# An attention layer in fp16 pairs: the low part of the attention result moves from VectorE to GpSimd

## What is computed

```
q, k, v = heads(x @ Wq + bq), heads(x @ Wk + bk), heads(x @ Wv + bv)
scores  = einsum('bhqd,bhkd->bhqk', q, k) / sqrt(32)
scores  = where(mask == 0, -inf, scores)
attn    = softmax(scores)
out     = einsum('bhqk,bhkd->bhqd', attn, v)      # back to (64, 128, 512)
result  = layernorm(x + out @ Wo + bo)            # eps 1e-5
```

## Time and profile before

| what | value |
|---|---|
| median of 3 runs | 910.06 us (909.27 to 911.1) |
| profiled execution | 910.95 us, its span 909.2 us |
| mean granted clock of PE | 0.986 of full speed |
| busy PE, DVE, ACT, POOL | 96%, 89%, 76%, 30% of the span |
| low part of the attention result on DVE (L463) | 44.7 us, 64 times, 698 ns |
| low part of x on POOL (L230) | 70.0 us, 60 times, 1166 ns |

### The profile page before, as it was taken

The page is one execution under the profiler, slowest core; times in us unless marked ns, Lnnn a source line. Parts: engine busy times, 40 slices in busy tenths (PEclk is TensorE's granted clock), DMA queues, the critical chain, the costliest instruction groups (busy, mean ns, idle before and its releaser), DMA issues.

```text
span 909.2 us, 34909 instructions
## 1 busy us (share of the span) xinstructions
PE 870.0 (96%) x11784; PEld 606.9 (67%) x11784; DVE 809.6 (89%) x3449; ACT 689.1 (76%) x1745; POOL 273.0 (30%) x386
## 2 busy tenths in 40 slices
PE   6989999999999999999999999999999999999954
PEld 4666667777666777666777666777766677766632
DVE  5789899989899999999999999998989999999984
ACT  5787788777787887777877778877778788777761
POOL 0122233332323333323333223333232333322222
PEclk9999999999999999999999999999999999999967
DMA  8277887876678877678877677787667887667863
GB/s 301 60 148 135 140 175 172 179 160 151 129 166 179 176 161 148 149 143 176 179 167 169 125 151 168 172 178 167 142 137 159 179 177 161 149 148 149 149 140 93
DMA packets 362287, 143.33 MB, mean 158 GB/s; under 512 B 340752, under 2 KB 344848, under 8 KB 361872
## 3 DMA queue, kind: packets, MB, share of 16 engines
q1 hardware_dynamic: 362256, 142.93, 73.3%
HBM read 42.21 MB, written 16.78 MB: 65 GB/s over the span
## 4 chain that ended last, share of the span: by engine, by line
PE 71%; DVE 21%; issue 4%; DMA 2%; DVEq 1%; ACT 0%; SPq 0%; POOL 0%; POOLq 0%; ACTq 0%
PE proj_ps L610 57%; PE score_ps L610 7%; PE av_ps L610 6%; DVE masked L497 6%; DVE p_pair L484 5%; DVE stats L526 3%; DVE y L523 3%; DVE qT_lo L477 1%; DVE v_parts L470 1%; DMA pT<-p_pair 1%; DVE minus_max L497 1%; DVE inv_sum L506 1%; DMA w_land<-weights 1%; DVE attn L511 0%; DMA aT<-a_pair 0%
## 5 line engine op out<-in xcount | busy, mean ns | idle before, releaser
L412 ACT ACTIVATE probs<-masked,minus_max 128x128 f32<-128x128 f32 x1024 | 326.9, 391 | 170.3 <-DVE minus_max L497 165.9
L497 DVE CUSTOM_DVE_ANT_0 masked<-score_ps,mask 128x128 f32<-128x128 f32 x1024 | 236.9, 287 | 48.2 <-PE score_ps L610 29.8
L484 DVE SCALAR_TENSOR_TENSOR p_pair<-probs,p_pair 128x512 f16<-128x512 f32 x256 | 196.6, 768 | 1.3 <-ACT p_pair L422 1.1
L422 ACT ACTIVATE p_pair<-probs 128x512 f16<-128x512 f32 x256 | 161.3, 630 | 13.3
L610 PE MATMUL proj_ps<-wo_hi,aT 128*128 128x512 f16 x512 | 166.4, 387 | 2.4 <-DMA aT<-a_pair 1.5
L230 POOL TENSOR_TENSOR xT_lo<-xT_raw,xT_hi 128x512 f16<-128x512 f32 x60 | 70.0, 1166 | 309.3 <-ACT xT_hi L375 309.3
L610 PE MATMUL proj_ps<-xT_hi,wq_hi 128*128 128x256 f16 x512 | 141.3, 276 | 11.3 <-DVE wq_lo L578 7.9
L610 PE MATMUL proj_ps<-xT_hi,wk_hi 128*128 128x256 f16 x512 | 140.3, 274 | 2.6 <-DVE qT_lo L477 2.4
L610 PE MATMUL proj_ps<-xT_lo,wq_hi 128*128 128x256 f16 x512 | 140.7, 275 | 0.0
L610 PE MATMUL proj_ps<-xT_hi,wq_lo 128*128 128x256 f16 x512 | 140.7, 275 | 0.0
L610 PE MATMUL proj_ps<-xT_hi,wk_lo 128*128 128x256 f16 x512 | 139.7, 273 | 0.0
(11 more groups left out here) (58 smaller groups left out, 1523.0 us busy)
## 6 DMA issues: line engine op xcount, KB each, us to landing
xT_raw<-x_cols SPq DMA_DIRECT2D x32, 512.0 KB, 4.3
x_in<-x_rows SPq DMA_DIRECT2D x32, 512.0 KB, 5.0
out<-y SPq DMA_DIRECT2D x64, 256.0 KB, 2.6
adj_in<-adj SPq DMA_DIRECT2D x32, 128.0 KB, 2.4
pT<-p_pair SPq DMA_TRANSPOSE x256, 3.1
w_land<-weights SPq DMA_DIRECT2D x2, 1024.0 KB, 7.7
w_land<-weights SPq DMA_DIRECT2D x4, 256.0 KB, 5.5
x_res<-weights SPq DMA_DIRECT2D x1, 1024.0 KB, 9.6
```

What stands on the lines that cost most here:

```text
L412: ins = act.activation(probs[s % 2][:, j * S:(j + 1) * S], masked[s % 2][:, j], ACT.Exp, bias=minus_max[s % 2][:, j:j + 1], scale=-1.0)
L422: act.activation(p_pair[s % NT][:, 0:HW], probs[s % 2][:], ACT.Copy, scale=P_UP).then_inc(p_hi_done, 1)
L484: dve.scalar_tensor_tensor(out=p_pair[s % NT][:, HW:2 * HW], in0=probs[s % 2][:], scalar=P_UP, in1=p_pair[s % NT][:, 0:HW], op0=ALU.mult, ...
L497: ins = dve.tensor_tensor_reduce(masked[s % 2][:, j], score_ps[j][:, s % HC], mask[par][:, s // KC], -EXP_SCALE, 3.0e38, ALU.add, ALU.min, ...
```

## The change

GpSimd makes the low part of the attention result. On GpSimd it stands at s=0 for the first graph and at s=4 for the second, and the second residual moves from s=4 to s=5. The constant column holds 1 instead of 16, so that the attention result comes out 16 times larger, and both of its parts are made without a multiplication: ACT copies without a scale, GpSimd subtracts.

```
+            def low_part_attn(g, b):
+                pool.wait_ge(a_hi_done, batch(g, b) + 1)
+                pool.tensor_tensor(a_pair[b][:, D:2 * D], attn[b][:], a_pair[b][:, 0:D],
+                                   ALU.subtract).then_inc(a_lo_done, 1)
...
                     if s == 1 and at_least(g, 2):
                         normalize(g - 2, 1)
+                    if s == 0 and at_least(g, 1):
+                        low_part_attn(g - 1, 0)
+                    if s == 4 and at_least(g, 1):
+                        low_part_attn(g - 1, 1)
...
-                    if s == 4:
+                    if s == 5:
                         residual(g, 1, par, k)
...
+            low_part_attn(LAST, 0)
             normalize(LAST - 1, 1)
+            low_part_attn(LAST, 1)
...
-                act.activation(a_pair[b][:, 0:D], attn[b][:], ACT.Copy, scale=UP).then_inc(a_hi_done, 1)
+                act.activation(a_pair[b][:, 0:D], attn[b][:], ACT.Copy).then_inc(a_hi_done, 1)
...
-            def low_part_attn(g, b):
-                dve.wait_ge(a_hi_done, batch(g, b) + 1)
-                dve.scalar_tensor_tensor(out=a_pair[b][:, D:2 * D], in0=attn[b][:], scalar=UP, in1=a_pair[b][:, 0:D],
-                                         op0=ALU.mult, op1=ALU.subtract).then_inc(a_lo_done, 1)
...
-                    if s in (2, 4) and at_least(g, 1):
-                        low_part_attn(g - 1, s // 4)
...
-                dve.memset(v_parts[i][:, :, :, V_ONE:VC], UP).then_inc(ones_made, 1)
+                dve.memset(v_parts[i][:, :, :, V_ONE:VC], 1.0).then_inc(ones_made, 1)
```

More of the change, by code:

```diff
@@ L597, in _ @@
             head_norm(LAST, SLOTS - 4)
-            low_part_attn(LAST, 0)
             y_and_moments(LAST - 1, 1, 1 - LAST % 2)
@@ L602, in _ @@
             head_norm(LAST, SLOTS - 1)
-            low_part_attn(LAST, 1)
             y_and_moments(LAST, 0, LAST % 2)
```

## The result

| | before | after |
|---|---|---|
| median of the runs, us | 910.52 (909.27 to 911.1, 4 runs) | 939.11 (936.53 to 940.44, 4 runs) |
| profiled execution, us | 910.95 | 940.44 |
| its span, us | 909.2 | 938.6 |
| mean granted clock | 0.986 | 0.986 |

The changed kernel is slower: the ratio of the times is 1.0312, 95% interval [1.0294, 1.0331]. That is 28.6 us between the medians and 29.5 between the profiled executions; the profiled one of the changed kernel is the slowest of its four, 1.3 above their median. The forecast was 21.3 us more, 932, with a range up to 935. The direction and the places were right, and the size was too small by 7 us.

What follows compares the result with a forecast made beforehand. PE was taken to set the pace, with DVE close behind. 14 passes x (0.55 + 0.92 + 0.07) = 21.6, plus 0.7, less 1.0, gave 21.3 us on the profiled 910.95: 932 us, range 916 to 935.

Steps and rivals of the forecast that it cites:

- the lead of 0.04: Second group, s=0: POOL starts at 487.31, DVE's L484 at 487.35, so POOL wins and L484 ends 0.98 late.
- the 44.7 us taken from DVE: 64 DVE instructions of 698 ns, in the loop at s=2 and s=4; removal costed at nothing there, hidden by PE's banks.
- the 20 us foretold: PE's waits for y at s=1 and Q0's low part at s=2, both groups: some 20 us in all.
- The rival in which the holds don't reach PE: L484's holds at s=0 cost 0 and only the end counts: 909.1 us; no holds or a gain, chance 0.07.
- The one in which DVE wins the second groups: Second groups, s=0: L484 keeps its time and POOL waits, cost 0 there: 918.5 us, chance 0.20.
- The rival "more than the sum": L484 held longer, or POOL's work slides onto a further L484, 0.35 to 0.98 each: 937 us, chance 0.06.
- the term for s=4: Both groups, s=4: L484 0.66 late against 0.60 of the moved instruction gone behind it, net 0.07 a pass.
- group 31's -1.0: Last group: 1.68 gained without the moved instruction, against a hold of 0.7 at s=0; net -1.0 us.
- the first groups' 0.55: First group, s=0: L484 held by POOL's low part ends 0.55 late, delaying PE's s=2; bounds 0 and 0.69.
- the second groups' 0.92: Second group, s=0: POOL wins, L484 ends 0.98 late, PE's s=2 starts at 493.62 instead of 492.70; cost 0.92.
- group 1 at 0 to 0.9: Group 1, where the pipeline still fills: taken at 0, bounds 0 to 0.9.
- Group 30: Like a second group, 0.92, but up to 0.86 comes back at s=2; taken at 0.7, bounds 0 to 0.9.

Runs made afterwards that it cites:

- the last experiment: POOL's long SBUF reads wait for DVE's L490: all, on the changed kernel, 907.75 and 906.76 us; only x's low parts, on the kernel before, 908.7 us.
- the run with one input: Kernel before plus a POOL multiply-add reading one SBUF tensor at s=0, behind one semaphore increment: 920.15 us, ratio 1.0076.
- one more subtraction: Kernel before plus one unused POOL subtraction of two SBUF tensors at s=0, low parts still on DVE: 935.2 us, ratio 1.0241.
- the kernel with the scale alone: Kernel before with constant column 1, ACT's copy without scale, and DVE making the low part as a plain subtraction: 910.62 us, ratio 0.9992.
- the kernels with the low parts behind L490: Changed kernel with POOL's two low parts of the attention result waiting for DVE's L490 of the same slot: 909.2 us, ratio 0.9978.
- the two kernels with a semaphore for each graph: Changed kernel with only the first graph's low part on POOL, 934.85 us, ratio 1.0248, or only the second's, 912.52 us, ratio 1.0002.
- All reads behind L490: Changed kernel with POOL's low parts of attention result and x, and first residual, waiting for L490 of their slot: 907.75 us (0.9944), again 906.76 (0.9933).
- the low parts of x alone behind: Kernel before with only POOL's low parts of x (s=3, 6) waiting for DVE's low part of the probabilities: 908.7 us, ratio 0.9949.

## Why the prediction was right in kind and too small

**Right.** POOL's start 0.08 behind ACT's end (475.81 against 475.89; 503.82 against 503.91), its 1.16, the hold with 0.55 behind POOL's end, the lead of 0.04 and that it decides, and y at s=1 as the place where it reaches PE: all are in the rows above. That the 44.7 us taken from DVE are worth nothing in the loop is shown by the last experiment, 53.65 to 53.66 us a pass without them on DVE and 53.66 with them. PE's waits for DVE came to the 20 us foretold (17.7 + 2.4). The rival in which the holds don't reach PE fell with 17.7 us of waits for y. The one in which DVE wins the second groups was a matter of 0.04 us, as the run with one input shows; that POOL won was read off a lead that an increment would have undone. The rival "more than the sum" gave 937, but not by what happened: no hold slid onto a further L490. In the loop those of s=0 and s=4 are held as foretold, those of s=3 and s=6, which POOL held before, by up to 0.1 more, and the others take 0.69.

**Too small.** The mechanism held and the sum did not. The step that failed is the term for s=4, "net 0.07" a pass with the bounds 0 and 0.07, which measured 0.20; group 31's -1.0 failed by the same reasoning, the first groups' 0.55 and the second groups' 0.92 were a little small (with one more subtraction alone they are 0.56 and 0.92, so what is above that is not the hold at s=0), and what came before the passes was set at 0. With the loop's four terms as measured, 4.4 us more, the forecast would have been 936.7. By stretch:

| term | predicted | measured | difference over the kernel |
|---|---|---|---|
| first group, s=0 and 1, a pass | 0.55 | 0.60 | 0.7 |
| second group, s=0 and 1, a pass | 0.92 | 1.00 | 1.1 |
| s=4, both groups, a pass | 0.07 | 0.20 | 1.8 |
| s=7, first group, a pass | 0 | 0.06 | 0.8 |
| first pass, on top of these | 0 | 0.37 | 0.4 |
| before the passes | 0 | 2.4 | 2.4 |
| groups 30 and 31 | -0.3 | 0.4 | 0.7 |

These add up to 7.9, against 29.4 - 21.3 = 8.1 of the spans. They are those of one execution of each kernel, and the 2.4 before the passes are not shown to come from the change, as is said below.

*s=4.* The prediction set the hold of 0.66 against the 0.60 of the instruction taken away (which is 0.06; it wrote 0.07), and did not look at the order of DVE's work. In the kernel before, DVE's timeline at s=4 goes on so:

```profile
474.43 0.87 DVE L477 SCALAR_TENSOR_TENSOR kT_lo<-proj_ps,b_qk_up,kT_hi 128x256 f16<-128x256 f32 x2
475.22 0.68 DVE L463 SCALAR_TENSOR_TENSOR a_pair<-attn,a_pair 128x512 f16<-128x512 f32 x1
```

and PE, at the next bank, before:

```profile
476.00 0.39 PE L610 MATMUL proj_ps<-wo_hi,aT 128*128 128x512 f16 x1
```

K1's low part, for which that bank waits, stands ahead of the moved instruction, so nothing was taken from its path. It ended at 475.30, 0.70 before the bank. Held by 0.66 it ends in the changed kernel at 491.53 + 0.86 = 492.39, and the bank starts 0.13 behind it:

```profile
492.52 0.39 PE L612 MATMUL proj_ps<-wo_hi,aT 128*128 128x512 f16 x1
```

The slack was 0.70 - 0.13 = 0.57, and 0.66 - 0.57 = 0.09 reach PE, in either group: 3.42 instead of 3.32. The bank of s=7 in first groups, 3.41 instead of 3.35, is another matter: the kernel with only the first low part on POOL has it too (3.41), and there nothing is held at s=4; the kernel with one more subtraction hardly has it (3.36), so it is not the hold at s=0 alone either. Its cause was not followed up.

*The first pass.* In both kernels one product of PE waits for a transpose there, 0.29 before (at 97.43) and 0.59 after (at 128.89), which makes a bank of 3.88 and one of 4.08; the kernel with the scale alone has no such wait and takes 53.85 for the pass. That difference is 0.1. Another 0.12 are at s=0 (4.08, in later passes 3.96), and 0.12 at s=1, which took 3.60 as in later passes, where the kernel before took 3.48 in its first pass and 3.60 later.

*The second group.* DVE's chain after the hold is what the prediction had, except that the normalization starts 0.29 behind the reciprocal (505.54, 505.83), where the kernels with the first low part alone on POOL and with one more subtraction have 0.20 and 0.21 in the same place, and their second group costs 0.92 exactly. So these 0.09 are not the hold. The normalizations at s=0 and s=4 are those that wait for `a_lo_done`, a semaphore that POOL, not DVE, counts up in the changed kernel. There, and in the kernels with the low parts behind L490, the step takes 0.29 to 0.33 in all four such places of a pass; in the kernel before only in the first group's s=0 (0.33, else 0.21), and in the two kernels with a semaphore for each graph nowhere (0.20 to 0.21). That points to how this wait is made, a part of the edit that the prediction put at nothing; no run changes it alone. With the low parts behind L490 the same 0.09 reach nobody.

*Before the passes, 2.4 us.* The first 0.75 lie ahead of the bank of group 1, in the stretch in which the weights arrive. Then that bank took 5.00 us instead of 3.34. Two stretches of the table by windows (us; busy and count of PE, PEld, DVE, ACT, POOL; granted clock; DMA share; GB/s), of the changed kernel:

```profile
54.00:56.00 2.00, 1.20 (x14) 0.82 (x7) 1.97 (x11) 1.97 (x5) 0.00 (x0) 0.73 0.60 115
56.00:58.00 2.00, 2.00 (x11) 1.44 (x10) 1.07 (x5) 1.89 (x6) 1.88 (x2) 0.50 0.48 89
```

and of the kernel before:

```profile
54.00:56.00 2.00, 1.85 (x17) 1.69 (x18) 1.97 (x13) 1.90 (x6) 0.00 (x0) 1.00 0.66 127
56.00:58.00 2.00, 2.00 (x42) 1.73 (x40) 0.52 (x3) 1.97 (x6) 0.00 (x0) 1.00 0.43 86
```

In the changed kernel PE's granted clock fell to the lower of its two levels (0.50 is 1.2 GHz) there, and in the kernel before it stayed at the higher. How busy PE was just ahead does not tell them apart: from 52 to 54 it was busy for 1.14 us of 2 in the changed kernel and for 0.64 in the kernel before, both at 1.00. The prediction took group 1 at 0 to 0.9 and thought of holds alone. Yet this is not tied to the hold: the kernels with the first low part alone on POOL (5.01 us), with the one-input read (4.81) and with the low parts behind L490, where none is held by them (4.87), show such a bank, while the kernel with one more subtraction, in which L490 is held in every pass, has 3.34, and so have those with the scale alone, the second low part alone and the memset.

Nor does the kernel settle it. All reads behind L490 was run twice, the same kernel to the letter, and each time one execution was traced. The stretch from 56 to 58 us in the first and in the second:

```profile
56.00:58.00 2.00, 2.00 (x20) 1.80 (x19) 1.97 (x12) 1.93 (x6) 0.30 (x1) 1.00 0.71 139
```

```profile
56.00:58.00 2.00, 2.00 (x12) 1.42 (x10) 1.37 (x7) 1.90 (x6) 0.94 (x1) 0.50 0.63 121
```

The first bank of group 1 took 3.34 us in the one and 5.00 in the other, that is, the 1.66 of the table come or stay away from one execution to the next. (A bank of group 0 was long in both, 7.60 and 7.55 us instead of 5.9, as it was, 7.60, with the low parts of x alone behind.) The stretch ahead of it scatters as well: group 1's first bank starts between 53.93 and 55.84 us in the twelve traces, at 55.84 and 55.20 in the two of one kernel. So the 2.4 us before the passes may be this one execution's and not the change's; that the profiled execution is 1.3 us above the median fits, and proves nothing. Whether the change makes the long bank more frequent is open.

*Groups 30 and 31.* Group 30 came as predicted, 0.57 against 0.7. In group 31, for which the prediction had -1.0, what failed is the same reasoning as at s=4: an instruction that goes was set against a hold, without asking which of them stands ahead of the one who waits. DVE's L490 of s=2, which the residual still holds, then SP's queue behind it (start, time in the queue), and PE's first bank of y in group 31, all of the changed kernel:

```profile
900.62 1.08 DVE L490 SCALAR_TENSOR_TENSOR p_pair<-probs,p_pair 128x512 f16<-128x512 f32 x1
```

```profile
899.38 3.71 SPq L258 DMA_TRANSPOSE pT<-p_pair  x2
903.27 1.24 SPq L267 DMA_TRANSPOSE aT<-a_pair  x1
```

```profile
906.53 0.59 PE L612 MATMUL proj_ps<-wo_hi,aT 128*128 128x512 f16 x1 [0.59 <-DMA aT<-a_pair]
```

Counted from the start of the bank of y before it (860.13 and 889.66), this L490 ends at 12.04, before at 11.31: 0.73 late, about the 0.7 that was set for the hold at s=0. The 1.68 that go stand behind it on DVE; the transposes stand behind it on SP, ahead of any gain. So the transpose of the attention result is issued 0.47 later than before (13.61 against 13.14 after that bank's start), though POOL's low part had been ready since 894.99, and the bank waits for it. It starts 0.2 earlier than before (16.87 against 17.07), and not 1.0. Behind that PE's banks of y run partly at the lower clock in both kernels, 5.27 us against 3.97 for this one, 7.04 against 8.22 for the two that end the kernel, which comes to 0.1 together (the bank between, 4.45 against 2.77, is made up for by shorter waits for transposes behind it). The group ends 0.1 earlier than before.

## What to carry to other kernels

Work handed to GpSimd was not free here though both engines had time. Lay each GpSimd instruction that reads SBUF where no VectorE instruction with two SBUF inputs is due. Where that can't be, try a wait that puts it behind that instruction; it cost nothing here, where nobody waited for GpSimd (a ratio of 0.9978 instead of 1.0312, and 0.9933 to 0.9944 when the reads that were there already got it too). When a hold is set against an instruction that goes, check in the order of the engine which of the two stands ahead of the consumer; the sum of the slot says nothing. And DVE, next to a PE that was busy 96% of the time, had no slack at all at two places of each pass: look for such places by the end of the producer against the start of the consumer, since a list of waits shows few of them. Last, one trace is one execution: a difference in a start-up stretch is worth a second trace of the same kernel before it gets a cause.

## What the runs showed of the hardware

- A 128x512 DVE instruction with two SBUF inputs that takes 0.69 us alone ended 0.54 to 0.56 us after the end of the POOL instruction that came before it, whatever its own start: 1.04, 1.25, 1.35 and 1.67 us. The reverse case cost POOL 0.5 us: 1.04 became 1.52 with one input, and 1.16 became 1.67 for a subtraction.
- The order was decided by 0.04 us in one direction (503.91 against 503.95, and 498.34 against 498.38) and by 0.07 in the other (494.07 against 494.00), the same within 0.01 in every second group of the loop. The instruction that stood behind one semaphore increment started 0.1 later, and its second groups lost nothing.
- A POOL memset beside the same DVE instruction, 0.39 us ahead of it, did not delay it (0.69), and the kernel with it took what the kernel before takes, 0.9994 [0.9979, 1.0009].
- Two executions of one kernel differed in PE's granted clock from 56 to 58 us, 1.00 and 0.50, and with it in the first bank of group 1, 3.34 and 5.00 us.
